# Layer 0 of a three-layer graph convolution sums its first 6 node tiles as dense count blocks

## The chip, the cores and the metric

The kernel runs on one core of a Trainium2 chip. The metric is the device time of one execution in microseconds, from which medians are taken. The engines are TensorE (PE, with its weight loads PEld), VectorE (DVE), ScalarE (ACT), GpSimd (POOL) and SyncE (SP), which issues plain DMAs.

## The reference

x has 6250 rows of 512 floats; `src` and `dst` list 106,250 edges (100,000 drawn ones and a loop at each node), sorted by `dst`. With deg the number of edges into a node and dinv = 1/sqrt(deg), each of three layers is

```python
msg = (h @ W)[src] * (dinv[src] * dinv[dst])[:, None]
h = segment_sum(msg, dst, n) + b
...
out = layernorm(x + h3)
```

The kernel uses that the layers are linear: y = dinv · h is summed over the edges, and W1·W2·W3 is applied as one product, once, at the end of layer 0. What remains of a layer is the sum of y[src] over each node's edges.

## The kernel before, in words

Nodes lie in 49 tiles of 128; `acc` holds them all in SBUF, and y of each layer is also stored in `y_dram`. A tile has about 16·128 = 2048 edges without its loops, and the loops are the start value of `acc`.

**Sparse sum.** The sorted edges are cut into 782 chunks of 128; 12 chunks make a group (66 groups) and 4 of them a quad (`CPQ`, 3 quads per group, `a` = 0, 1, 2). For each chunk POOL gathers 128 rows of y by an indirect DMA (line 808, `gather`), into a ring of 5 quads; `gather_quad(n)` waits until the quad 5 before is summed. PE multiplies a one-hot block of 32 columns with the gathered rows (`sum_quad`, line 1019), four chunks into four strips of one bank. After a group's last quad ACT copies the bank (`copy_slots`, line 1280), PE places the 128 rows by another one-hot product (`place_group`, line 1030), and DVE adds them, masked, to the two tiles that the group may touch (`add_group`, line 1648). DVE stages the one-hots: `stage_places` (line 1622, five quads ahead) and `stage_group` (line 1628).

**Dense sum.** In layers 1 and 2 the first 17 tiles are summed otherwise. `a_dram` holds for each of them a block of counts (uint8, how many edges go from each source node to each of the tile's nodes). A unit (`dense_unit`, line 1109) multiplies count blocks of 4 source tiles with their y rows, each row split in a high and a low float32r part (`high_part` on ACT, `low_part` on DVE, line 1789); ACT widens the counts (`widen_a`, line 1308), DVE adds the result to `acc` (`add_unit`, line 1800). Source tiles come back from `y_dram` by SP's loads (`load_y`, `load_a`). So in these layers only the groups from 22 on are gathered: 518 chunks, 131 quads.

**The count blocks are built in layer 0.** 272 windows of 8 nodes, 16 per tile: DVE stages two pairs of bf16 one-hots (`stage_window`, lines 1769 and 1770), PE multiplies them (`build_window`, line 1083), ACT copies the result into the tile's block (`keep_windows`, line 1288), SP stores the block (`store_a`). They are spread over quads 22 to 192 (`window_quad`), two build banks in turn. Ahead of them DVE finds the windows' edges, POOL gathers these (`gather_windows`, 6 indirect DMAs before the 14th quad), DVE turns them into values (`value_windows`, lines 1735 to 1753, at quad 17), and PE transposes these.

**Tiles of layer 0.** As a tile's last group is added, PE transposes it (`turn_done_tile`, line 1038), ACT copies it, PE multiplies it with W1·W2·W3 (`multiply_tile`, line 1054), DVE adds the bias (`bias_rows`, line 1656), ACT scales it (`scale_rows`, line 1248), and SP stores it. The last two tiles come after the loop (`last_tiles`). Layer 1's gathers wait until all tiles are stored.

**Order.** Every engine runs a list that is written out by quad: PE's `first_layer` in layer 0 does the sum of the quad, the placement of the group before, transposes, product, windows (line 1125); ACT's, DVE's and SP's have the same form (lines 1335, 1831, 695). An engine does its list in order, and each step waits on semaphores for its inputs; `FINISH` gives the quads of the tiles. Before the layer PE multiplies the weights (line 951) and turns the edge lists (`turn_lines`); `keep_groups` on DVE ends with the masks (`groups_ready`), for which POOL's first gather waits. Before quad 4 POOL waits for the weights and writes two constants (`window_consts`, line 812).

## Time and profile before

| | us |
|---|---|
| median of 3 runs | 2594.88 |
| lowest, highest | 2591.75, 2608.73 |
| profiled execution: span from first to last instruction | 2590.5 |
| profiled execution: its own time around the span | not recorded |
| layer 0, first to last gather | 137.4 to 1133.7 |
| layer 1, first gather | 1166.1 |

The profiled execution's own time is not among the results; its span is 1.2 us under the fastest of the three runs. Times in the profile are microseconds unless marked ns; PE, DVE, ACT, POOL and SP are the engines; an arrow points from what is read to what is written; the text behind an arrow in brackets names what ended an idle time.

### The profile page before, as it was taken

The numbers are of one execution on the slowest core, as the hardware profiler recorded it, in microseconds if no ns is written. First come the engines' busy times: TensorE is split into PE (matmuls) and PEld (weight loads), VectorE is DVE, ScalarE is ACT, GpSimd is POOL, SyncE is SP. The second block draws the span as 40 slices with busy tenths as digits, with TensorE's granted clock in tenths as the row PEclk, the third lists the DMA queues.
The fourth block names the chain that finished last, engine by engine and source line by source line (L and its number), as shares of the span: only waits on it lengthen the run. The fifth ranks groups of instructions, "written<-read, shape, count | busy, mean of one in ns | idle before, by whom it ended". The sixth has DMA issues, their size and how long they took to land. (4 is left out here: it accounts for less than half of the span.)

```text
span 2590.5 us, 30320 instructions
## 1 busy us (share of the span) xinstructions
PE 2035.3 (79%) x9476; PEld 998.1 (39%) x9476; DVE 1301.1 (50%) x3394; ACT 689.0 (27%) x1287; POOL 1767.1 (68%) x1864
## 2 busy tenths in 40 slices
PE   6565776777777767768998989998798888988854
PEld 6311222222222222225555555554355555555421
DVE  8323454445444544435444444445555555555577
ACT  0500222222222222223323223333322232223221
POOL 0267777777777777737777777777577776676652
PEclk9766888888878888889999999999899999999886
DMA  7667777777777778748888888889788888788784
GB/s 259 228 176 202 231 236 235 233 244 236 233 244 234 235 233 245 233 148 257 267 264 259 262 266 266 264 261 299 230 263 270 254 264 261 239 259 258 243 265 146
DMA packets 270364, 628.29 MB, mean 243 GB/s; under 512 B 46275, under 2 KB 99456, under 8 KB 270208
## 3 DMA queue, kind: packets, MB, share of 16 engines
q0 software_dynamic: 146256, 478.35, 61.3%
q1 hardware_dynamic: 123952, 148.03, 16.8%
q8 instruction: 77, 1.26, 0.2%
q14 instruction: 79, 0.65, 0.1%
HBM read 560.77 MB, written 65.45 MB: 242 GB/s over the span
## 5 line engine op out<-in xcount | busy, mean ns | idle before, releaser
L808 POOL DMA_INDIRECT ring<-y_dram,kept x1818 | 1741.0, 958 | 682.6 <-issue 575.1
L1019 PE MATMUL ps<-ring,onehot 128*32 128x512 f32 x3636 | 553.6, 679 | 302.6 <-DMA ring<-y_dram,kept 302.2
L1109 PE MATMUL ps<-dense_first,wide_a 128*128 128x512 f32 x1700 | 507.6, 421 | 49.5 <-DVE acc L1800 33.0
L1800 DVE SCALAR_TENSOR_TENSOR acc<-ps,acc 128x512 f32<-128x512 f32 x442 | 305.0, 690 | 360.1 <-PE ps L1109 350.4
L1109 PE MATMUL ps<-dense_next,wide_a 128*128 128x512 f32 x1224 | 382.1, 423 | 66.3 <-ACT wide_a L1308 39.0
L1109 PEld LDWEIGHTS ps<-dense_first,wide_a 128*128 128x128 f32 x1700 | 323.4, 196 | 218.9 <-issue 100.6
L1308 ACT CAST wide_a<-onehot 128x512 fp32r<-128x512 uint8 (+1 forms) x442 | 258.0, 594 | 372.9 <-PE ps L1109 366.5
L1622 DVE TENSOR_TENSOR onehot<-ps,kept 128x128 f32<-128x128 f32 x459 | 131.5, 287 | 412.8 <-PE ps L1019 412.7
L1109 PEld LDWEIGHTS ps<-dense_next,wide_a 128*128 128x128 f32 x1224 | 230.7, 194 | 202.9 <-issue 83.9
L1019 PEld LDWEIGHTS ps<-ring,onehot 128*32 128x32 f32 x3636 | 81.8, 113 | 498.8 <-issue 487.4
L1648 DVE SCALAR_TENSOR_TENSOR acc<-ps,mask,acc 128x512 f32 x308 | 217.0, 746 | 72.4 <-issue 67.4
L1769 DVE TENSOR_SCALAR onehot<-onehot 128x128 bf16<-128x128 bf16 x544 | 142.6, 262 | 192.6 <-PE ps L1083 192.2
L1280 ACT COPY onehot<-ps 128x512 f32<-128x512 f32 (+1 forms) x154 | 90.1, 585 | 556.1 <-PE ps L1019 556.1
L1054 PE MATMUL ps<-w,w_sb 128*128 128x512 f32 x376 | 220.5, 740 | 0.0
L1288 ACT CAST ring<-ps 128x392 uint8<-128x392 f32 x272 | 125.9, 486 | 316.6 <-PE ps L1083 314.6
L1030 PE MATMUL ps<-onehot 128*128 128x512 f32 (+1 forms) x308 | 190.8, 704 | 22.2 <-ACT onehot L1280 13.8
L1770 DVE TENSOR_SCALAR ring<-onehot 128x392 bf16<-128x392 bf16 x544 | 184.3, 339 | 0.0
L1083 PE MATMUL ps<-ring,onehot 128*128 128x392 bf16 x544 | 136.3, 358 | 31.9 <-DVE ring L1770 29.9
L1054 PEld LDWEIGHTS ps<-w,w_sb 128*128 128x128 f32 x376 | 86.6, 244 | 158.2 <-issue 158.2
L1109 PE MATMUL ps<-dense_last,wide_a 128*128 128x512 f32 x408 | 132.0, 406 | 0.0
L1248 ACT ACTIVATE acc<-h_sb,dinv 128x512 f32<-128x512 f32 x96 | 69.4, 722 | 191.2 <-DVE h_sb L1656 191.2
L1030 PEld LDWEIGHTS ps<-onehot 128*128 128x128 f32 (+1 forms) x308 | 49.8, 203 | 167.2 <-issue 167.2
(237 smaller groups left out, 1034.0 us busy)
## 6 DMA issues: line engine op xcount, KB each, us to landing
ring<-y_dram,kept POOLq DMA_INDIRECT x1818, 4.3
onehot<-a_dram SPq DMA_DIRECT2D x408, 64.0 KB
y_dram<-acc SPq DMA_DIRECT2D x99, 256.0 KB, 3.8
a_dram<-ring SPq DMA_DIRECT2D x17, 784.0 KB, 5.6
acc<-in_x_dram SPq DMA_DIRECT2D x1, 12288.0 KB
y_dram<-acc SPq DMA_DIRECT2D x12, 1024.0 KB, 10.8
ring<-y_dram SPq DMA_DIRECT2D x48, 256.0 KB, 4.8
out_dram<-row_sb SPq DMA_DIRECT2D x48, 256.0 KB
```

What stands on the lines that cost most here:

```text
L808: pool.indirect_dma_start(ring[:, s, :], None, y_dram[layer], bass.IndirectOffsetOnAxis(ap=rows, axis=0)).then_inc(done, 16)
L1019: mm = pe.matmul(ps[k * WIDE:(k + 1) * WIDE, g % BANKS, :], wide_hot[:, r, k, :], ring[:, r * CPQ + k, :], start=opens, stop=closes, tile_ ...
L1030: pe.matmul(ps[:, PLACE_BANK, :], place_hot[0:rows, g % 2, :], slots[0:rows, g % 2, :], start=True, stop=True).then_inc(placed, 1)
L1054: mm = pe.matmul(ps[:, PRODUCT_BANK, :], turned_sb[:, k * P:(k + 1) * P], w123[:, k, :], start=(k == 0), stop=(k == FB - 1))
L1083: mm = pe.matmul(ps[:, BUILD_BANKS[w % 2], 0:WIDTH], lo_hot[:, w % 2, h, :], v_hot[:, w % 2, h, :], start=(h == 0), stop=(h == 1))
L1109: mm = pe.matmul(ps[:, bank, :], wide_a[:, n % WIDE_SLOTS, P * k:P * (k + 1)], y_parts[(TILES * (layer - 1) + tile) % YSLOTS][:, part, :], ...
L1308: act.copy(wide_a[:, n % WIDE_SLOTS, 0:width], a_slots[n % ASLOTS][:, 0:width]).then_inc(a_ready, 1)
L1622: dve.tensor_tensor(wide_hot[:, n % RING_QUADS, :, :], iota_ps[:, 0:WIDE].unsqueeze(1).broadcast_to([P, CPQ, WIDE]), lo_f[:, c:c + CPW * ( ...
L1648: dve.scalar_tensor_tensor(out=rows, in0=ps[:, PLACE_BANK, :], scalar=mask[:, part, own:own + 1], in1=rows, op0=ALU.mult, op1=ALU.add).the ...
L1769: dve.tensor_scalar(lo_hot[:, w % 2, h, :], v_iota[:, HALF:HALF + P], lo_cols[:, at:at + 1], None, ALU.is_equal)
L1770: one = dve.tensor_scalar(v_hot[:, w % 2, h, :], v_iota, v_cols[:, at:at + 1], None, ALU.is_equal)
L1800: dve.scalar_tensor_tensor(out=rows, in0=ps[:, DENSE_BANKS[n % 2], :], scalar=0.5, in1=rows, op0=ALU.mult, op1=ALU.add).then_inc(dense_add ...
```

## The change

Layer 0 now sums its first 6 tiles (`EARLY_DENSE`) as dense count blocks as well, and gathers only from group 7 on: 698 chunks, 59 groups, 176 quads. To that end:
- The windows of these 6 tiles (96) are built first, three per quad in quads 11 to 42, the other 176 in quads 44 to 169. What leads to them is moved ahead: masks at quad 2 (was 5), search at 4 (was 8), window gathers before quad 10 (was 14), values at quad 8 (was 17). There is one build bank (5) in place of two, since the banks 3 and 6 go to the units. The first window of a quad stands before the quad's sum, the second behind it.
- 150 units (`dense0_unit`): 24 pairs of source tiles and a last single one, times 6 tiles, in quads 49 to 151. y rows are read back in pairs from `y_dram` (49 loads of 256 KB), count blocks in rows of 256 bytes (150 loads, 4 slots); ACT makes the high part and widens, DVE makes the low part and adds (`add0_unit`).
- The 6 tiles are finished at quads 151 to 161, and tiles finish at least two quads apart. The product of a tile uses the bank of its transposes, so `turn_done_tile` waits for the bias row before.
- The first 3 groups get masks of their own (`mask0`), which leave out what belongs to the 6 tiles; PE's weight products now stand behind a product that waits for `groups_ready`.
- b3 is loaded at the start of layer 1 in place of the start of the kernel, some SBUF regions are laid out anew, and the size of POOL's DMA scratch is given as 8192 bytes.

```diff
 DENSE_SPARE = 700
+EARLY_DENSE = 6
+PAIR = 2
+Y0_SLOTS = 4
+A0_SLOTS = 4
+WIDE0_SLOTS = 2
...
-    FIRST = [0, DENSE_GROUPS, DENSE_GROUPS]
...
-    WIN_AT = 22
-    WIN_QUADS = LAYER_QUADS[0] - WIN_AT - 4
+    WIN_AT = 11
+    WIN_PACE = 3
+    EARLY_WINDOWS = EARLY_DENSE * WPT
+    REST_AT = WIN_AT + EARLY_WINDOWS // WIN_PACE + 1
+    REST_QUADS = LAYER_QUADS[0] - REST_AT - 6
+    PAIRS0 = (TILES + PAIR - 1) // PAIR
+    UNITS0 = PAIRS0 * EARLY_DENSE
+    UNITS0_FROM = REST_AT + 5
+    UNITS0_TO = LAYER_QUADS[0] - 6 - 3 * EARLY_DENSE
...
+    def pair_of(b):
+        return range(PAIR * b, min(PAIR * b + PAIR, TILES))
+    UNIT0_QUAD = [UNITS0_FROM + (UNITS0_TO - UNITS0_FROM) * u // UNITS0 for u in range(UNITS0)]
+    LOAD0_QUAD = [UNITS0_FROM - 4 if b < 2 else UNIT0_QUAD[(b - 1) * EARLY_DENSE - 1] + 1 for b in range(PAIRS0)]
+    SPLIT0_QUAD = [UNITS0_FROM - 2 if b < 2 else LOAD0_QUAD[b] + 1 for b in range(PAIRS0)]
+    def units0_at(q):
+        return [u for u in range(UNITS0) if UNIT0_QUAD[u] == q]
+    def splits0_at(q):
+        return [k for k in range(TILES) if SPLIT0_QUAD[k // PAIR] == q]
...
     def finish_quads(layer):
-        dense = DENSE if layer > 0 else 0
-        sparse = [(first_quad(layer, LAST_GROUP[t] + 1) + (2 if layer == 0 else 0), 0, t) for t in range(dense, LOOP_TILES)]
-        return sorted(sparse + [(UNIT_QUAD[layer][UNITS - DENSE + t] + 1, 1, t) for t in range(dense)])
+        if layer > 0:
+            sparse = [(first_quad(layer, LAST_GROUP[t] + 1), 0, t) for t in range(DENSE, LOOP_TILES)]
+            return sorted(sparse + [(UNIT_QUAD[layer][UNITS - DENSE + t] + 1, 1, t) for t in range(DENSE)])
+        ready = sorted([(first_quad(0, LAST_GROUP[t] + 1) + 2, 0, t) for t in range(EARLY_DENSE, LOOP_TILES)]
+                       + [(UNIT0_QUAD[UNITS0 - EARLY_DENSE + t] + 3, 1, t) for t in range(EARLY_DENSE)])
+        found, at = [], -2
+        for q, late, t in ready:
+            at = max(q, at + 2)
+            found.append((at, late, t))
+        return sorted(found)
...
     def window_quad(w):
-        return WIN_AT + WIN_QUADS * w // WINDOWS
+        if w < EARLY_WINDOWS:
+            return WIN_AT + w // WIN_PACE
+        return REST_AT + REST_QUADS * (w - EARLY_WINDOWS) // (WINDOWS - EARLY_WINDOWS)
...
+            def load_y0(k):
+                if k == 0:
+                    sp.wait_ge(y0_stored, 16 * (X_BATCHES + 1))
+                    sp.wait_ge(win_values, 1)
+                if units0_before(k) > 0:
+                    sp.wait_ge(dense0_done, units0_before(k))
+                sp.dma_start(y0_raw[k % Y0_SLOTS], node_rows(y_dram[0], k, 0, P)).then_inc(y0_loaded[k % Y0_SLOTS], 16)
+            def load_a0(u):
+                b, t = divmod(u, EARLY_DENSE)
+                if u == 0:
+                    for k in range(2):
+                        sp.wait_ge(a_stored[k], 16 * ((EARLY_DENSE + 1 - k) // 2))
+                if u >= A0_SLOTS:
+                    sp.wait_ge(a0_ready, u - A0_SLOTS + 1)
+                width = P * len(pair_of(b))
+                sp.dma_start(a0_slots[u % A0_SLOTS][:, 0:width],
+                             a_dram[P * t:P * (t + 1), P * PAIR * b:P * PAIR * b + width]).then_inc(a0_loaded[u % A0_SLOTS], 16)
+            def load_dense0(q):
+                for b in range(PAIRS0):
+                    if LOAD0_QUAD[b] == q:
+                        for k in pair_of(b):
+                            load_y0(k)
+                if q == UNITS0_FROM - 2:
+                    for u in range(A0_SLOTS):
+                        load_a0(u)
+                for u in range(A0_SLOTS, UNITS0):
+                    if UNIT0_QUAD[u - A0_SLOTS] == q:
+                        load_a0(u)
             def store_a(q):
...
                     window_consts()
-                if n == WIN_AT - 8:
+                if n == WIN_AT - 1:
...
                 mm.then_inc(slots_ready, 1)
+                pe.wait_ge(first_ready, 1)
+                pe.wait_ge(groups_ready, 1)
+                pe.matmul(ps[:, GROUP_BANK, FIRST_AT:FIRST_AT + BOUNDARY], ones[0:1, :], first_tiles[0:1, :],
+                          start=True, stop=True).then_inc(first_spread, 1)
             def sum_quad(n):
...
             def turn_done_tile(t):
-                pe.wait_ge(added, 2 * (LAST_GROUP[t] + 1))
-                if t > 0:
-                    pe.wait_ge(turn_copied, t)
+                turn = TURN_OF[0][t]
+                if t < EARLY_DENSE:
+                    pe.wait_ge(dense0_added, UNITS0 - EARLY_DENSE + t + 1)
+                    pe.wait_ge(added, 2 * BOUNDARY)
+                else:
+                    pe.wait_ge(added, 2 * (GROUP.index((0, LAST_GROUP[t])) + 1))
+                if turn > 0:
+                    pe.wait_ge(turn_copied, turn)
+                    pe.wait_ge(h_ready, turn)
...
             def build_window(w):
                 pe.wait_ge(win_hot, w + 1)
-                if w > 1:
-                    pe.wait_ge(win_kept, w - 1)
+                if w > 0:
+                    pe.wait_ge(win_kept, w)
                 for h in range(2):
-                    mm = pe.matmul(ps[:, BUILD_BANKS[w % 2], 0:WIDTH], lo_hot[:, w % 2, h, :], v_hot[:, w % 2, h, :], start=(h == 0), stop=(h == 1))
+                    mm = pe.matmul(ps[:, BUILD_BANK, 0:WIDTH], lo_hot[:, w % 2, h, :], v_hot[:, w % 2, h, :], start=(h == 0), stop=(h == 1))
                 mm.then_inc(win_built, 1)
             def build(q):
-                if q == 7:
+                if q == 3:
                     sum_starts()
-                if q == WIN_AT - 4:
+                if q == WIN_AT - 2:
                     turn_windows(0)
-                if q == WIN_AT - 3:
+                if q == WIN_AT - 1:
                     turn_windows(1)
-                for w in windows_at(q):
-                    build_window(w)
+            def dense0_unit(u):
+                b, t = divmod(u, EARLY_DENSE)
+                bank = DENSE_BANKS[u % 2]
+                tiles = pair_of(b)
+                if t == 0:
+                    pe.wait_ge(split0_ready, tiles[-1] + 1)
+                pe.wait_ge(a0_ready, u + 1)
+                if u >= 2:
+                    pe.wait_ge(dense0_added, u - 1)
+                for k, tile in enumerate(tiles):
+                    for part in (y0_high, y0_low):
+                        mm = pe.matmul(ps[:, bank, :], wide0[:, u % WIDE0_SLOTS, P * k:P * (k + 1)], part[tile % Y0_SLOTS],
+                                       start=(k == 0 and part is y0_high), stop=(k == len(tiles) - 1 and part is y0_low))
+                mm.then_inc(dense0_done, 1)
...
                     g, a = QUAD[q]
+                    windows, units = windows_at(q), units0_at(q)
+                    for w in windows[:1]:
+                        build_window(w)
                     sum_quad(q)
+                    for w in windows[1:2]:
+                        build_window(w)
                     if a == 0 and q > 0:
                         place_group(g - 1)
                     for t in finished_at(0, q + 1):
                         turn_done_tile(t)
                     for t in finished_at(0, q):
-                        multiply_tile(t)
+                        multiply_tile(TURN_OF[0][t], TURN_BANK)
                     build(q)
+                    for w in windows[2:]:
+                        build_window(w)
+                    for u in units:
+                        dense0_unit(u)
             def last_tiles(layer):
                 place_group(GROUP_AT[layer + 1] - 1)
...
+                pe.wait_ge(dense0_added, UNITS0)
+                pe.wait_ge(h_ready, LOOP_TILES)
...
                 act.copy(y_parts[n % YSLOTS][:, 0, :],
                          y_rows[n % YSLOTS][:, 1, :] if tile > 0 else tile_of(source(0))).then_inc(high_ready, 1)
+            def high0(k):
+                act.wait_ge(y0_loaded[k % Y0_SLOTS], 16 * (k // Y0_SLOTS + 1))
+                if units0_before(k) > 0:
+                    act.wait_ge(dense0_done, units0_before(k))
+                act.copy(y0_high[k % Y0_SLOTS], y0_raw[k % Y0_SLOTS]).then_inc(high0_ready, 1)
+            def widen_a0(u):
+                width = P * len(pair_of(u // EARLY_DENSE))
+                act.wait_ge(a0_loaded[u % A0_SLOTS], 16 * (u // A0_SLOTS + 1))
+                if u >= WIDE0_SLOTS:
+                    act.wait_ge(dense0_done, u - WIDE0_SLOTS + 1)
+                act.copy(wide0[:, u % WIDE0_SLOTS, 0:width], a0_slots[u % A0_SLOTS][:, 0:width]).then_inc(a0_ready, 1)
             def widen_a(layer, u):
...
+                    windows = windows_at(q)
+                    for k in splits0_at(q):
+                        high0(k)
+                    keep_windows(windows[:1])
                     if q + 1 == QUADS_TO[g]:
                         copy_slots(g)
                     for t in finished_at(0, q + 1):
-                        keep_turned(t)
-                    keep_windows(q)
+                        keep_turned(TURN_OF[0][t])
+                    keep_windows(windows[1:])
+                    for u in units0_at(q + 1):
+                        widen_a0(u)
                     for t in finished_at(0, q):
-                        scale_rows(0, t)
+                        scale_rows(0, t, h_sb, TURN_OF[0][t])
...
+                                             scalar=float(EARLY_DENSE - part), in1=mask[:, part, EARLY_GROUPS:EARLY_GROUPS + BOUNDARY],
+                                             op0=ALU.is_ge, op1=ALU.mult).then_inc(mask0_ready, 1)
+                dve.wait_ge(mask0_ready, 2)
             def invert_degrees(twice):
...
+                    near = mask0[:, part, g:g + 1] if g < BOUNDARY else mask[:, part, own:own + 1]
+                    dve.scalar_tensor_tensor(out=rows, in0=ps[:, PLACE_BANK, :], scalar=near,
                                              in1=rows, op0=ALU.mult, op1=ALU.add).then_inc(added, 1)
             def bias_rows(layer, t, h=h_sb, bank=PRODUCT_BANK, turn=None):
...
             def build(q):
-                if q == 5:
+                if q == 2:
                     window_masks()
-                if q == 8:
+                if q == 4:
                     find_windows()
-                if q == WIN_AT - 5:
+                if q == WIN_AT - 3:
                     value_windows()
-                if q in (WIN_AT - 4, WIN_AT - 3):
-                    keep_columns(q - (WIN_AT - 4))
+                if q in (WIN_AT - 2, WIN_AT - 1):
+                    keep_columns(q - (WIN_AT - 2))
                 for w in windows_at(q + 1):
                     stage_window(w)
...
+                dve.wait_ge(high0_ready, k + 1)
+                dve.tensor_tensor(y0_low[k % Y0_SLOTS], y0_raw[k % Y0_SLOTS], y0_high[k % Y0_SLOTS].bitcast(F32),
+                                  ALU.subtract).then_inc(split0_ready, 1)
+            def add0_unit(u, groups):
+                dve.wait_ge(dense0_done, u + 1)
+                if groups > 0:
+                    dve.wait_ge(added, 2 * groups)
+                if u > 0:
+                    dve.wait_ge(dense0_added, u)
+                rows = tile_of(u % EARLY_DENSE)
+                dve.scalar_tensor_tensor(out=rows, in0=ps[:, DENSE_BANKS[u % 2], :], scalar=0.5, in1=rows,
+                                         op0=ALU.mult, op1=ALU.add).then_inc(dense0_added, 1)
             def add_unit(layer, u, groups):
...
                     g, a = QUAD[q]
+                    for u in units0_at(q - 1):
+                        add0_unit(u, g - (1 if a == 0 else 0))
                     finish_quad(q)
                     if a == 0 and q > 0:
                         add_group(g - 1)
                     build(q)
                     for t in finished_at(0, q):
-                        bias_rows(0, t)
+                        bias_rows(0, t, h_sb, TURN_BANK, TURN_OF[0][t])
+                    for k in splits0_at(q):
+                        low0(k)
             def last_tiles(layer):
...
-    nc = bacc.Bacc("TRN2", target_bir_lowering=False, num_devices=1)
+    nc = bacc.Bacc("TRN2", target_bir_lowering=False, num_devices=1, dynamic_dma_scratch_size=8192)
```

## Rows read from the trace of the kernel before

**Rows 1.** The page: busy time, share of the span and instructions of each engine.
```profile
PE 2035.3 (79%) x9476; PEld 998.1 (39%) x9476; DVE 1301.1 (50%) x3394; ACT 689.0 (27%) x1287; POOL 1767.1 (68%) x1864
```

**Rows 2.** Stretches: us, busy of PE, PEld, DVE, ACT, POOL, clock, DMA share, GB/s.
```profile
300.00:1100.00 800.00, 586.88 (x2339) 182.20 (x2340) 369.02 (x1354) 195.64 (x381) 607.40 (x633) 0.83 0.78 237
1200.00:1700.00 500.00, 455.28 (x2185) 271.84 (x2183) 238.61 (x427) 150.65 (x259) 379.24 (x397) 1.00 0.85 262
1700.00:1800.00 100.00, 88.60 (x427) 52.30 (x428) 51.82 (x92) 36.36 (x61) 75.75 (x80) 1.00 0.88 280
```

**Rows 3.** The gathers of line 808 in layer 0, and its waits (us, times).
```profile
L808 POOL DMA_INDIRECT ring<-y_dram,kept x782: 942/946/1627, 137.4 to 1133.7; - x196
...
  issue: 234.4, 770
...
  PE ps L1019: 3.4, 11
```

**Rows 4.** The gathers' wait for PE in layer 1 (us, times).
```profile
  PE ps L1019: 8.8, 29
```

**Rows 5.** The chain that ended last, in layer 2: start us, us, what.
```profile
1878.39 1.06 PE ps L1030 x2
...
1886.14 1.00 PE ps L1019 x8
1887.13 3.86 PE ps L1109 x16
```

**Rows 6.** Timeline, end of layer 0, PE: start us, us, engine line op.
```profile
1101.76 0.66 PE L1038 MATMUL ps<-ident,acc 128*128 128x128 f32 x4
...
1121.57 3.70 PE L1054 MATMUL ps<-w,w_sb 128*128 128x512 f32 x8
...
1125.11 0.83 PE L1083 MATMUL ps<-ring,onehot 128*128 128x392 bf16 x4
```

**Rows 7.** DVE lines of layer 1: count, min/median/max ns, first and last start.
```profile
L1800 DVE SCALAR_TENSOR_TENSOR acc<-ps,acc x197: 678/692/693, 1201.5 to 1797.7; 128x512 f32<-128x512 f32 x197
...
L1789 DVE TENSOR_TENSOR dense_first<-ring,dense_first x21: 680/684/766, 1216.5 to 1740.1; 128x512 fp32r<-128x512 f32 x21
```

**Rows 8.** Timeline, end of layer 0, DVE and ACT.
```profile
1088.19 0.24 DVE L1769 TENSOR_SCALAR onehot<-onehot 128x128 bf16<-128x128 bf16 x1
...
1088.59 0.24 DVE L1769 TENSOR_SCALAR onehot<-onehot 128x128 bf16<-128x128 bf16 x1
...
1127.10 0.28 DVE L1622 TENSOR_TENSOR onehot<-ps,kept 128x128 f32<-128x128 f32 x1
...
1128.03 0.35 DVE L1628 TENSOR_SCALAR onehot<-ps,kept 128x128 f32<-128x128 f32 x1 [0.65 <-PE ps L1030]
...
1128.36 0.48 ACT L1288 CAST ring<-ps 128x392 uint8<-128x392 f32 x1 [0.42 <-PE ps L1083]
...
1128.77 1.41 DVE L1648 SCALAR_TENSOR_TENSOR acc<-ps,mask,acc 128x512 f32 x2 [0.39 <-issue]
```

**Rows 9.** Timeline, start of layer 0.
```profile
133.81 16.34 PE L951 MATMUL ps<-ring 128*128 128x512 f32 x32
...
157.15 0.49 POOL L812 IOTA row_sb<- 128x392 f32 x1
...
240.92 0.55 DVE L1735 TENSOR_SCALAR ring<-ring 128x768 int32<-128x768 int32 x1
...
249.79 0.96 DVE L1753 TENSOR_TENSOR ring<-ring 128x768 f32<-128x768 f32 x1
```

**Rows 10.** Timeline, first gather of layer 1.
```profile
1166.12 0.94 POOL L808 DMA_INDIRECT ring<-y_dram,kept  x1 [31.47 <-issue]
```

**Rows 11.** DMA queues in layer 1 (packets, MB, share), and the count-block loads.
```profile
q0 software_dynamic: 36769, 120.51, 67.5%
q1 hardware_dynamic: 37998, 31.85, 17.1%
...
onehot<-a_dram SPq DMA_DIRECT2D x189, 64.0 KB
```

96 lines of the change are left out of this document (74 added, 22 removed).

## The prediction

> **What bounds the kernel now.** I read the engine totals first [rows 1]: PE is busiest with 79%, POOL second with 68%. That is an average over three layers, so next the table of stretches [rows 2]. The reader is to see that POOL does the same in both layers shown: 633 gathers in the 800 us of layer 0, 397 in 500 us and 80 in 100 us of layer 1, one per 1.26 us each time, although PE is 73% busy in the first and 91% in the second. Then line 808 alone [rows 3]. Its 782 gathers of layer 0 start between 137.4 and 1133.7 us. Nearly all its idle time (234.4 us over 770 gaps, 0.30 us each) is called issue: the gap of an engine that waits for nothing. It waits for PE (a free ring slot) 11 times, at most 0.3 us. So a gather costs 0.946 + 0.30 = 1.25 us, POOL never rests, and layer 0 is as long as its list of gathers. Layer 1 shows the same bound beside fuller PE work: between 1170 and 1800 us 29 waits for PE, 8.8 us in all [rows 4].
>
> **What is removed.** Layer 0 starts at group 7 (its first 6 tiles hold (128·16·6 − 700)/1536 = 7 whole groups), so 7 groups, 21 quads and 7·12 = 84 gathers go: 782 become 698, 197 quads become 176. Seven place products and fourteen additions go with them. At the pace of rows 3, (1133.7 − 137.4)/787 = 1.266 us per gather (781 steps and the 6 window gathers), stretches included: 84 · 1.266 = 106.3 us. All of it is on the path, if POOL stays the engine that never rests.
>
> **What is added, in PE time per quad.** A quad of four gathers lasts 4 · 1.266 = 5.06 us; this is the budget. The 150 units lie on quads 49 to 151, 1.46 per quad.
> - A unit is 4 products (2 source tiles, high and low part; 2 for the last block). 16 cost 3.86 us in layer 2 [rows 5], so 0.97 us; 1.41 us per quad.
> - Sum of the quad 1.00, a placement 1.07 per three quads, 0.36 [rows 5].
> - A tile's product 3.70 and its transposes 0.66 [rows 6], one tile per some 3.9 quads: 1.12.
> - Windows: two take 0.83 us [rows 6], 0.42 each; 176 over 126 quads, 1.4 per quad: 0.58.
> The sum is 1.00 + 0.36 + 1.12 + 0.58 + 1.41 = 4.47 us of 5.06, or 88%. Layer 1 runs at 91% PE busy and holds the pace of the gathers [rows 2], so the products as such fit.
>
> **DVE per quad:** 1.46 unit additions of 0.69 and half a low part of 0.68 [rows 7], 1.3; windows, two pairs of 0.40 each [rows 8], 1.4 · 0.80 = 1.1; one group addition per three quads, 0.65 + 0.35 + 0.39 + 1.41 [rows 8], 0.93; places 0.3, and a bias row like a unit addition, every 3.9 quads, 0.2. That is 3.9 of 5.06 us. It fits too, but DVE and PE are in order and hand work to each other, and here I expect the loss.
> - Quads 49 to 151: the first window of a quad is now built ahead of the sum. PE stands at it until DVE has staged it, and DVE stages it only after the group addition. Counted from the end of the units before: window 0.4, sum 1.0, place 1.07, to 2.5 us; DVE then 0.4 + 0.35 + 0.39 + 1.41 + 0.8, to 5.8 us; PE's own units end at 4.0. So PE idles 1.8 us in each group's first quad, unless a tile's product lies there. Behind the waiting window are the quad's sum and with it POOL's free slot. Three quads then need 3 · 4.47 + 1.8 = 15.2 us, and POOL gives them 15.2. This is break-even: I charge 0.05 us per quad over 103 quads, 5 us; bounds 0 (the tile's product fills the gap) and 0.3 per quad, 31 us.
> - Quads 11 to 42 carry three windows each (96 in 32 quads), and there is one build bank in place of two: each build waits for ACT's copy of the one before (0.48 us [rows 8]). Window w+2 needs the hot buffer of w, so DVE stages the last one only when PE has begun the next quad. By the same count a quad without a group takes 3.3 us, one with a group 6.6, and a tile's product adds 4.4 in four of five groups of quads: 16.7 per three, 5.6 each, 0.5 over the budget, 17 us in 32 quads. The ring of 5 quads absorbs some: a sum ends some 10 us after its first gather and its slot is wanted after 25, so PE may be 15 us late. It has about 7 us of lag already (next point). That leaves 17 + 7 − 15 = 9 us; bounds 0 and 24.
> - The window gathers move from the 14th to the 10th quad, and the values are wanted at quad 8. DVE will wait for their landing and then works 9.8 us (240.92 to 250.75 [rows 9]), with PE behind it at the transposes. The 6 gathers go out to about 196 us and land by 200, values are ready at 210, and POOL next needs a slot at about 221: nothing lost, but 7 us of lag.
> - Start: PE now waits for groups_ready before the weight products. These ran from 133.8 to 150.2 and would run from about 137 to 153.5; POOL asks for them at 157.15, before its IOTA [rows 9]. Hidden; without that cover 3 us. The small copies and masks on DVE lie before onehots wanted 5 us later; the one copy ahead of the masks costs 0.1 us. b3's load leaves the start and goes ahead of layer 1's tile loads: 0.4 us on SP, not on POOL's path.
> - End of layer 0: POOL stands 31.5 us until the last rows are stored [rows 10]. The last tile is finished at the same distance from the end (173 of 176, before 194 of 197), and the six early tiles at 151 to 161, before it. Same gap; I take 0, bounds −3 and +5.
> - SP: 49 tile loads and 150 count-block loads are queued with the stores of the tiles. They are issued two quads or more before use, 10 us; what is late next is ACT's widening. I charge 2 us, bounds 0 and 10.
>
> **DMA.** In layer 1, 461 gathers took 67.5% of 580 us, 0.85 us of all 16 engines each; the other queue took 17.1%, 99 us, for 189 count blocks (12.4 MB) and, from the rest of its 31.85 MB, 74 transfers of 256 KB. These at 0.85 are 63 us, which leaves 0.19 us per count block [rows 11]. Added in quads 49 to 151 (515 us): 49 · 0.85 + 150 · 0.19 = 70 us, a share of 0.14 on 0.78 [rows 2]: 0.92, where the rows hold the pace up to 0.88. I cost it at 0 in the sum; at the other end, a ceiling of 0.88 gives 515 · (0.92/0.88 − 1) = 23 us.
> The count blocks of layer 0 are read 256 bytes at a time, those of layer 1 512. The Trainium skill, DMA: Bandwidth & Descriptors, Specifications, says that below 512 bytes the engines read, modify and write and line rate is lost. No row here shows the two sizes apart. As a mechanism of this kernel, doubling the 0.19 gives 28 us more, a share of 0.98, and 515 · (0.98/0.88 − 1) = 58 us.
>
> The last edit gives POOL's queue 8192 bytes for its descriptors in place of the default. No row shows how many gathers either size holds. Four quads are under way at most and one gather lands while some four are issued, so I take 0; were it too small, POOL would wait for landings in all three layers, and one more gap of 0.30 us on 1734 gathers would be 520 us. I give that end 0.01 (in C's share).
>
> **Sum.** Against the profiled execution's span: 2590.5 − 106.3 + 5 + 9 + 2 = 2500. What lies around the span is not shown; the fastest run is 1.2 us above it and the median 4.4. I add 3: **2503 us**. Layers 1 and 2 keep their code; 0 there.
>
> **Rivals.**
> - A, DMA is the limit in quads 49 to 151. For it: shares rise to 0.92 or 0.98 with this traffic, and the ring has little room for later landings if PE lags as well. Against it: 0.88 held 80 gathers per 100 us [rows 2], and 84 gathers are gone. 2590.5 − 106 + 3 + (23 to 58), with the lock-step beside it: 2520 to 2550, say 2530.
> - B, TensorE stays at the mixed clock. It was granted 0.83 in layer 0 and 1.00 in layer 1 [rows 2]. PE's 587 us in 800 is 3.7 us per quad where the full clock's rows give 3.2: a factor of 1.15. Then 4.47 becomes 5.1, with the waits 5.6 us per quad, 0.55 · 103 = 57 us: 2545. Against it: idle waits for rows are what separates the layers, and these shrink.
> - C, slower than before: the one build bank. If every window's copy and its signals (0.48 + 0.4 us) stand open on PE instead of beside a sum or a product, PE needs 4.47 + 1.4 · 0.88 = 5.7 us per quad over 126 quads (+81), and 5.6 + 2.6 in the early 32 (+100): with 106 saved about 2590 + 75 = 2665. The change loses from about 0.67 us open per window on. For it: ACT's queue holds copies and widenings ahead of the next copy. Against it: the code puts the first window before the sum and the second behind it.
> - D, the gain is whole (the ring hides all): 2487.
>
> **Chances.** Forecast 0.55 (its own range 2492 to 2520), D 0.15, A 0.13, B 0.10, C 0.07. The range from 2482 to 2552 leaves out C and the edges of the others. One per cent is 26 us, about what a measurement of this kernel can tell from no change: faster by more than that (under 2569) are the forecast, D, A and most of B, 0.91; within, 0.04; slower 0.05.
>
> **What would show it.** Right: 698 gathers of line 808 in layer 0 at 1.25 to 1.29 us, the last at about 1042; the clock near 1.00 from quad 49 on; POOL waiting for PE some 10 us about 250 to 400 us and little later; PE waiting at the window product for DVE; the gap to layer 1 near 31 us. Wrong: gathers at 1.35 us or more in the second half of layer 0 with a DMA share at 0.9 (A), or with PE at 95% and a clock under 0.9 (B); PE idle on the build bank after ACT's window copy (C).

## The result, and the profile after

| us | before | changed | forecast |
|---|---|---|---|
| median | 2602.14 (6 runs) | 2577.57 (6 runs, 2568.29 to 2606.05) | 2503 (2482 to 2552) |
| ratio | | 0.9935 [0.9907, 0.9963] | 0.965 |
| profiled span | 2590.5 | 2603.8 | 2500 |
| last gather of layer 0 starts | 1133.7 | 1136.3 | 1042 |
| first gather of layer 1 starts | 1166.1 | 1170.1 | 1073.5 |

The kernel gains 0.65% by the ratio on record in place of 3.5%; the two medians in the table, divided, give 0.9906. The profiled execution is the slowest of its six, 28 us above their median. The lines of the new kernel that answer to [rows 3]: its gathers (line 919) of layer 0, with the first eight of layer 1, and the last two starts around the gap.

```profile
L919 POOL DMA_INDIRECT ring<-y_dram,kept x706: 940/946/2272, 137.6 to 1178.9; - x177
...
  issue: 195.7, 642
  PE ps L1134: 124.6, 62
```

```profile
1136.31 0.94 POOL L919 DMA_INDIRECT ring<-y_dram,kept  x1 [3.79 <-PE ps L1134]
1170.14 0.94 POOL L919 DMA_INDIRECT ring<-y_dram,kept  x1 [32.89 <-DMA y_dram<-acc]
```

84 gathers are gone, and the last one still starts 2.6 us later than before. A gather itself costs the same (0.946 + 0.30 us), so the new size of POOL's DMA scratch costs nothing that shows. What is new is 124.6 us in 62 waits for PE's sum to free a ring slot; before there were 3.4 us in 11. POOL no longer sets the pace.

Where that happens is read from the starts of every fourth gather (a quad has four), in us per quad; PE's busy and idle share of the same quads stand beside it, from its instructions in the trace.

| kernel | quads 20 to 49 (PE busy + idle) | quads 49 to 157 (PE busy + idle) | last gather |
|---|---|---|---|
| before | 5.09 (3.69 + 1.40) | 5.06 (3.70 + 1.36) | 1133.7 |
| changed | 7.18 (5.04 + 2.14) | 5.45 (4.53 + 0.92) | 1136.3 |

(7.18 − 5.09) · 29 = 61 us and (5.45 − 5.06) · 108 = 42 us: 103 us, nearly all of the 106 that was to be gained. The stretches behind it, before and changed in turn (us, busy of PE, PEld, DVE, ACT, POOL, clock, DMA share, GB/s):

```profile
225.00:420.00 195.00, 139.13 (x562) 44.33 (x558) 93.58 (x312) 42.64 (x82) 148.18 (x154) 0.84 0.77 230
480.00:960.00 480.00, 355.25 (x1413) 110.77 (x1414) 223.96 (x825) 118.47 (x230) 364.53 (x380) 0.83 0.78 236
```

```profile
225.00:420.00 195.00, 136.72 (x475) 40.64 (x474) 98.01 (x383) 50.66 (x101) 108.86 (x114) 0.74 0.62 184
480.00:960.00 480.00, 400.85 (x1778) 182.68 (x1776) 303.68 (x852) 166.51 (x362) 340.27 (x351) 0.94 0.81 249
```

In the first stretch (three windows per quad) PE is as busy as before and does a quarter fewer sums; the clock fell to 0.74. In the second (the units) the clock rose to 0.94, where near 1.00 was forecast, and the DMA share is 0.81. PE's and POOL's waits in these stretches (us, times, longest), first 225 to 420, then 480 to 960:

```profile
PE ps L1204 <- ACT ring L1436: 33.9, 35, 1.9
PE ps L1204 <- DVE ring L1953: 24.4, 9, 3.8
POOL ring L919 <- PE ps L1134: 56.1, 22, 6.9
...
PE ps L1204 <- DVE ring L1953: 59.2, 35, 2.8
PE ps L1204 <- ACT ring L1436: 19.1, 15, 5.6
PE ps L1227 <- DVE acc L1989: 0.7, 2, 0.4
POOL ring L919 <- PE ps L1134: 39.7, 22, 5.8
```

PE waits nearly always at one place, the window product (line 1204): for DVE's one-hots (line 1953), and for ACT's copy out of the one bank (line 1436). The units themselves (line 1227) wait 0.7 us in 480. One round of three early quads on PE (start, us, line, wait before), and the stretches in it by clock (the clock is the first number behind POOL's brackets):

```profile
284.34 1.06 PE L1134 MATMUL ps<-ring,onehot 128*32 128x512 f32 x8
...
285.68 1.02 PE L1145 MATMUL ps<-onehot 128*128 128x512 f32 x2
...
289.73 0.83 PE L1204 MATMUL ps<-ring,onehot 128*128 128x392 bf16 x2 [2.70 <-DVE ring L1953]
290.49 1.94 PE L1134 MATMUL ps<-ring,onehot 128*32 128x512 f32 x8
292.36 0.84 PE L1204 MATMUL ps<-ring,onehot 128*128 128x392 bf16 x2
292.99 1.06 PE L1159 MATMUL ps<-ident,acc 128*128 128x128 f32 x4
295.20 0.81 PE L1204 MATMUL ps<-ring,onehot 128*128 128x392 bf16 x2 [1.16 <-ACT ring L1436]
296.68 0.81 PE L1204 MATMUL ps<-ring,onehot 128*128 128x392 bf16 x2 [0.67 <-ACT ring L1436]
297.43 1.94 PE L1134 MATMUL ps<-ring,onehot 128*32 128x512 f32 x8
...
299.92 4.99 PE L1175 MATMUL ps<-w,w_sb 128*128 128x512 f32 x8
...
305.91 0.49 PE L1204 MATMUL ps<-ring,onehot 128*128 128x392 bf16 x2 [0.67 <-ACT ring L1436]
306.33 1.07 PE L1134 MATMUL ps<-ring,onehot 128*32 128x512 f32 x8
```

```profile
284.34:289.10 4.76, 2.69 (x15) 0.78 (x14) 3.15 (x10) 1.46 (x3) 3.70 (x4) 1.00 0.80 235
289.10:302.70 13.60, 11.15 (x34) 3.52 (x35) 6.57 (x29) 3.50 (x7) 8.24 (x9) 0.50 0.71 217
302.70:309.50 6.80, 4.28 (x19) 1.35 (x19) 2.61 (x10) 1.58 (x3) 2.92 (x4) 1.00 0.45 120
```

From sum to sum of the same place in the group the round takes 22.0 us, where POOL would need 15.2. The place product at 285.68 opens the longest wait: DVE adds the group only then, and stages the next window behind that. During that wait of 2.70 us the granted clock fell from 1.00 to 0.50 and came back at 302.7: the two sums in between take 1.94 us each in place of 1.06, and the tile's product, more than half of its time at the low clock, 4.99 in place of 3.70. The sum at 306.33 takes 1.07 us again, although PE waited 0.67 us just before it.

### The profile page after: what moved, and what is told of

It reads as the page before. It is cut to its first block and busy times, and to the rows that moved or that the text cites. A ratio compares the mean times of both kernels' runs of the same rounds, so it can differ in the third digit from the quotient of the medians.

```text
span 2603.8 us, 32039 instructions
## 1 busy us (share of the span) xinstructions
PE 2122.2 (82%) x9884; PEld 1096.7 (42%) x9884; DVE 1421.8 (55%) x3556; ACT 761.5 (29%) x1479; POOL 1688.9 (65%) x1780
## 5 line engine op out<-in xcount | busy, mean ns | idle before, releaser
L919 POOL DMA_INDIRECT ring<-y_dram,kept x1734 | 1662.8, 959 | 775.0 <-issue 508.4
L1134 PE MATMUL ps<-ring,onehot 128*32 128x512 f32 x3468 | 517.7, 666 | 75.9 <-DMA ring<-y_dram,kept 75.4
L1244 PE MATMUL ps<-dense_first,wide_a 128*128 128x512 f32 x1700 | 515.3, 426 | 53.3 <-DVE acc L2000 32.4
L1204 PE MATMUL ps<-ring,onehot 128*128 128x392 bf16 x544 | 159.6, 380 | 187.7 <-DVE ring L1953 118.5
L1830 DVE SCALAR_TENSOR_TENSOR acc<-ps,mask,acc 128x512 f32 x294 | 207.2, 746 | 78.5 <-issue 73.6
L1145 PE MATMUL ps<-onehot 128*128 128x512 f32 (+1 forms) x294 | 178.2, 690 | 20.2 <-ACT onehot L1428 13.9
L1204 PEld LDWEIGHTS ps<-ring,onehot 128*128 128x128 bf16 x544 | 35.9, 101 | 362.2 <-DVE ring L1953 224.7
L1134 PEld LDWEIGHTS ps<-ring,onehot 128*32 128x32 f32 x3468 | 74.4, 112 | 256.8 <-issue 250.6
L1175 PE MATMUL ps<-w,w_sb 128*128 128x512 f32 x376 | 182.0, 629 | 0.0
L1809 DVE TENSOR_SCALAR onehot<-ps,kept 128x128 f32<-128x128 f32 x147 | 51.4, 350 | 141.3 <-PE ps L1145 141.1
```

The source lines that it names most:

```text
L919: pool.indirect_dma_start(ring[:, s, :], None, y_dram[layer], bass.IndirectOffsetOnAxis(ap=rows, axis=0)).then_inc(done, 16)
L1134: mm = pe.matmul(ps[k * WIDE:(k + 1) * WIDE, g % BANKS, :], wide_hot[:, r, k, :], ring[:, r * CPQ + k, :], start=opens, stop=closes, tile_ ...
L1145: pe.matmul(ps[:, PLACE_BANK, :], place_hot[0:rows, g % 2, :], slots[0:rows, g % 2, :], start=True, stop=True).then_inc(placed, 1)
L1175: mm = pe.matmul(ps[:, bank, :], turned_sb[:, k * P:(k + 1) * P], w123[:, k, :], start=(k == 0), stop=(k == FB - 1))
L1204: mm = pe.matmul(ps[:, BUILD_BANK, 0:WIDTH], lo_hot[:, w % 2, h, :], v_hot[:, w % 2, h, :], start=(h == 0), stop=(h == 1))
L1244: mm = pe.matmul(ps[:, bank, :], wide_a[:, n % WIDE_SLOTS, P * k:P * (k + 1)], y_parts[(TILES * (layer - 1) + tile) % YSLOTS][:, part, :], ...
```

## The experiments

Each kernel is the changed kernel with the edit that is shown; e0 and e11 are without one. A pace is the time per quad, for quads 20 to 49 and 49 to 157. The runs e0 to e3 were made on one chip (before: 2594.53 us median), f1 to f3 on another with 2595.59 us. For e4 to e7 the kernel before took 2945.69 us, for e8 to e11, on a third chip, 2942.88 us; these eight are compared by their ratios alone.

**e0: the changed kernel again.**

> The changed kernel once more, as it is. It was 0.65% faster than the kernel before (0.9935), and its profiled execution was the longest of its six. Theory H (hand-overs): in layer 0 POOL waits for PE because PE stands for ACT's window copy (one build bank), for DVE's staging and behind ACT's wait for y rows. Then this profile shows again over 6.5 us per quad while quads 11 to 44 are summed and 5.3 to 5.5 us in the units' quads. Rival L (luck): the 105 us that went missing belong to that one slow execution, and this profile shows layer 0 at 5.1 us per quad and the last gather near 1030 us. Time by H: 2565 to 2580 us, by L the same here but with the profile 80 us shorter in layer 0.

Measured: 2588.76 us (12 runs, 2574.70 to 2601.49), 0.9977 [0.9958, 0.9997]. Paces 7.06 and 5.42: the loss is there again, at a median somewhat above the 2565 to 2580 us expected. By the two ratios the change is worth 0.2 to 0.65%.

**e1: two banks for the 96 early windows.**

```
+        def build_bank(w):
+            return 6 if w < EARLY_WINDOWS and w % 2 == 0 else BUILD_BANK
-                if w > 0:
+                if 1 < w < EARLY_WINDOWS:
+                    pe.wait_ge(win_kept, w - 1)
+                elif w > 1:
                     pe.wait_ge(win_kept, w)
...
```

(PE's product and ACT's copy take `build_bank(w)` in place of `BUILD_BANK`.)

> The first 96 windows are built in two banks in turn (bank 5 and bank 6, which the units take only from quad 49 on), so that a build waits for the copy of the window two before. Theory bank: PE stood 33.9 us for ACT's copy between 225 and 420 us, at a clock of 0.74; without that the early stretch falls from 7.1 to about 6 us per quad, 30 us shorter, 2545 us. Rival staging: DVE's staging behind the group addition and PE's low clock set the pace of the early stretch, and the waits only move to DVE: 0 to 10 us shorter. Rival DMA predicts no change.

Measured: 2534.40 us (2530.74 to 2536.19), 0.9765 [0.9750, 0.9781]. Stretch 225 to 420, and the window products in it (count, busy, mean ns of one, idle before them):

```profile
225.00:420.00 195.00, 150.15 (x662) 50.61 (x660) 129.95 (x494) 66.82 (x141) 148.38 (x154) 0.89 0.81 250
```

```profile
L1210 PE MATMUL ps<-ring,onehot 128*128 128x392 bf16 x202 | 55.0, 367 | 45.8 <-DVE ring L1959 30.4 <-ACT ring L1442 15.5
```

The early quads are back at 5.09 us with 154 gathers, as many as before; those from 49 on stay at 5.38, as they must. The second bank gives 54 us against e0, where about 30 were expected, and by the paces nearly all of it early (57 us, and 4 later). Not all of it is time spent waiting for the bank: the granted clock of the stretch is 0.89 in place of 0.75 too. DVE's waits did not shrink (30.4 us, 23.4 in e0, over more quads), so they alone did not make the early loss.

**e2: y rows split two quads after their load in place of one.**

```
-    SPLIT0_QUAD = [UNITS0_FROM - 2 if b < 2 else LOAD0_QUAD[b] + 1 for b in range(PAIRS0)]
+    SPLIT0_QUAD = [UNITS0_FROM - 2 if b < 2 else LOAD0_QUAD[b] + 2 for b in range(PAIRS0)]
```

> The high and low parts of a pair of y rows (from the third pair on) are made one quad later, two quads after their load is issued instead of one. Theory load: ACT stands at the landing of the y rows (31 us in all between 480 and 960 us, up to 4.7 us at a time), with the copy of the quad's first window behind it and PE behind that (19.1 us of waits for the copy, 5.6 at most). Then these waits go and the units' quads fall by 15 to 25 us in all, 2550 to 2560 us. Rival staging: the loss in the units' quads is PE's 59 us of waits for DVE's window staging; then 0 to 5 us. Rival transfer limit: the loads land late because the DMA engines are full, and the waits stay with a quad more or less: 0.

Measured: 2567.20 us (2556.63 to 2588.66), 0.9918 [0.9889, 0.9946]. What it acts on, ACT and PE of the changed kernel:

```profile
708.65 0.62 ACT L1454 CAST x_rows<-w_sb 128x512 fp32r<-128x512 f32 x1 [4.66 <-DMA w_sb<-y_dram]
712.22 0.62 ACT L1454 CAST above_dense<-w_sb 128x512 fp32r<-128x512 f32 x1 [2.95 <-DMA w_sb<-y_dram]
712.74 0.48 ACT L1436 CAST ring<-ps 128x392 uint8<-128x392 f32 x1
```

```profile
706.21 0.51 PE L1204 MATMUL ps<-ring,onehot 128*128 128x392 bf16 x2 [1.80 <-DVE ring L1953]
...
713.36 0.81 PE L1204 MATMUL ps<-ring,onehot 128*128 128x392 bf16 x2 [5.65 <-ACT ring L1436]
```

ACT stands at a y row that has not landed, with the copy of a window that PE built 6.5 us earlier queued behind it, and PE stands at the bank. With the later split PE's waits for ACT between 480 and 960 us fall from 20.4 (e0) to 4.3 us, and the pace from 5.42 to 5.32: 11 us over 108 quads, between the two expectations (15 to 25, 0 to 5). The rest of e2's gain isn't the edit's. Its quads 20 to 49 hold the same instructions as e0's and ran at 6.21 in place of 7.06; see the last section.

**e3: DVE stages the next quad's first window ahead of the group addition.**

```
...
+                    early = windows_at(q + 1)[:1] if q >= WIN_AT else []
+                    for w in early:
+                        stage_window(w)
                     if a == 0 and q > 0:
                         add_group(g - 1)
-                    build(q)
+                    build(q, len(early))
```

> DVE stages the first window of the next quad ahead of the addition of a finished group, from quad 11 on; the rest of its order is kept. Theory staging: PE stands at a quad's first window for DVE (24.4 us between 225 and 420 us in 9 waits, 59.2 us between 480 and 960 us in 35), behind the group addition of about 2.9 us; these waits fall to a third, and the time by 40 to 60 us, to 2520 to 2535 us. Rival bank: the early stretch keeps its pace, since PE then stands for ACT's copy: 15 to 25 us. Rival load: no more than 10 us.

Measured: 2504.78 us (2501.81 to 2507.36), 0.9654 [0.9639, 0.9669]. The two stretches, then POOL's waits in the second:

```profile
225.00:420.00 195.00, 137.81 (x598) 44.37 (x598) 117.66 (x462) 64.15 (x129) 136.01 (x141) 0.90 0.75 231
480.00:960.00 480.00, 421.36 (x1922) 189.66 (x1914) 323.03 (x923) 177.66 (x389) 365.00 (x378) 0.96 0.85 266
```

```profile
POOL ring L919 <- PE ps L1134: 0.6, 2, 0.3
```

(`build` then leaves out what is staged already.) Six changed lines that add no instruction give 84 us back against e0, more than the 40 to 60 us expected. PE's waits for DVE's one-hots in 480 to 960 fall from 59.2 (e0) to 14.1 us; those for ACT's copy rise from 20.4 to 35.5 us and do no harm. From quad 49 on the pace is 5.09: 378 gathers in 480 us against 380 before, POOL waits for PE 0.6 us, and DMA at a share of 0.85 holds that. The early quads go from 7.06 to 5.66, at a clock of 0.90 in place of 0.75.

**f1: PE builds the first window behind the quad's sum.** It tests the step of the prediction by name: is it the sum that stands behind a late window?

```
-                    for w in windows[:1]:
-                        build_window(w)
                     sum_quad(q)
+                    for w in windows[:1]:
+                        build_window(w)
```

> The changed kernel, with the first window of a quad behind the quad's sum on PE instead of ahead of it; DVE's order and the one bank stay. If the loss is the sum, and with it POOL's free slot, standing behind a window product whose one-hots DVE stages late (theory 1 as the prediction put it), the quads from 49 on fall from 5.4 to about 5.1 us (108 quads, some 35 us) and the early ones from 7.1 by the 1 us or so that PE stands there per quad: 2520 to 2550 us, ratio 0.97 to 0.98. If it is the length of the whole round (the place product behind the windows, the group addition behind the place product, the staging behind that), the order on PE only shifts it: early quads stay at 7 us or more and the ratio within 0.99 to 1.00; it may rise, since two windows then stand back to back on one bank.

Measured: 2552.05 us (2542.29 to 2562.77), 0.9822 [0.9790, 0.9853]. PE's and POOL's waits, 225 to 420 and 480 to 960:

```profile
PE ps L1204 <- ACT ring L1436: 44.0, 38, 2.9
PE ps L1204 <- DVE ring L1953: 11.6, 9, 1.8
POOL ring L919 <- PE ps L1134: 49.7, 19, 4.4
...
PE ps L1204 <- ACT ring L1436: 39.5, 36, 5.8
PE ps L1204 <- DVE ring L1953: 28.2, 29, 2.5
POOL ring L919 <- PE ps L1134: 7.2, 11, 3.1
```

The two theories share the layer between them. From quad 49 on (5.17 in place of 5.42) POOL's wait goes from 39.7 to 7.2 us: there the sum behind the window was the loss, as the step said. In the early quads (6.85 in place of 7.06, 0.2 us where 1 was expected) DVE's waits only turned into ACT's and POOL still loses 49.7 us: there the whole round is too long, and this order on PE does not mend it.

**f2: two banks, and staging ahead** (the edits of e1 and e3 together).

> Two banks for the early windows and staging ahead of the group addition. If the two losses are separate, quads 20 to 49 run at 5.1 us where staging alone left 5.66: 16 us below it, ratio 0.959 where the kernel before takes 2595 us (2489 us). If staging alone already frees what the bank cost (the 5.66 being a slower clock or lag): ratio 0.965. Where the kernel before takes some 2945 us, 0.973 to 0.978 as measured there, and (b) stays open.

Measured: 2496.47 us (2495.65 to 2498.28), 0.9622 [0.9604, 0.9641], the fastest of all; it beats both kernels.

```profile
225.00:420.00 195.00, 142.04 (x657) 48.46 (x655) 124.79 (x488) 66.80 (x142) 148.99 (x152) 0.93 0.80 248
480.00:960.00 480.00, 419.55 (x1910) 187.81 (x1909) 322.28 (x921) 176.14 (x384) 365.06 (x378) 0.96 0.85 264
```

```profile
PE ps L1138 <- DMA ring<-y_dram,kept: 23.9, 15, 6.6
PE ps L1210 <- ACT ring L1442: 16.1, 17, 1.3
PE ps L1210 <- DVE ring L1959: 12.9, 18, 1.9
...
POOL ring L923 <- PE ps L1138: 0.9, 3, 0.3
```

Quads 20 to 49 run at 5.15, 49 to 157 at 5.09, and PE's sums wait for gathered rows again, as before (waits of 225 to 420 us). The layer is bound by POOL's list once more. The ratio lies between the two that were expected (0.959, 0.965). The two gains overlap: 54 and 84 us alone, about 92 together (0.9977 − 0.9622 of 2595). The paces against e0 say where: in the early quads 57 (e1), 41 (e3) and 55 us (f2), in the later ones 4, 36 and 36. The early loss is mended by either edit, most of all by the bank, the later one by the staging alone; and 5.06 us per quad, POOL's own pace before, is the floor of both.

**f3: staging ahead, and the first window behind the sum.**

> Staging ahead of the group addition, and the first window behind the sum on PE; one bank. If staging ahead is what pays and PE's order is then without weight: ratio 0.965 as with staging alone. If the window ahead of the sum was useful (it gives the one bank's copy the whole sum to hide behind), the early quads rise from 5.66 to 6 us or more: 10 us or more above, ratio 0.969 or higher.

Measured: 2504.52 us, 0.9657 [0.9637, 0.9678]; paces 5.57 and 5.10, as e3. Once DVE stages ahead, the order on PE has no weight that can be told.

**e4 to e11, where every kernel was 13% slower.**

e6 copies the second window ahead of ACT's copies of a transposed tile; e7 builds two early windows per quad:

```
+                    keep_windows(windows[1:2])
                     for t in finished_at(0, q + 1):
                         keep_turned(TURN_OF[0][t])
-                    keep_windows(windows[1:])
+                    keep_windows(windows[2:])
...
-    WIN_PACE = 3
+    WIN_PACE = 2
```

e4 and e8 are f2's kernel, e5 and e9 add e2's edit to it, e10 is e3's and e6's edit with one bank, e11 the changed kernel.

> The two early build banks and the earlier staging of a quad's first window together. Apart they gave 0.9765 and 0.9654 of the time before. Theory hand-overs: bank and staging are the whole early loss, staging alone the loss in the units' quads; then quads 20 to 49 go at 5.1 us and the later ones at 5.1, the last gather starts near 1030 us, 2488 us. Rival, DMA as a limit: beside the units a pace of 5.2 us or more stays however well the engines hand over, 2500 us. Rival, one remedy makes the other moot: no better than the earlier staging alone, 2505 us.

> The three edits together: two early banks, earlier staging, high and low parts a quad later. Theory hand-overs: POOL never waits long in layer 0, the whole 106 us of the gathers appear, 2485 us, equal to the two edits together within 3 us, since the ring hides ACT's waits for y rows once PE has slack. Rival load: ACT's waits for the rows (35.5 us on PE, 7.2 at most, with the earlier staging) still cost, and this kernel beats the two edits by 5 to 10 us.

> The changed kernel with one swap on ACT: it copies a quad's second window before the turned tile, as PE makes them in that order. One build bank stays. Theory bank: PE's waits for ACT in the early stretch (33.9 us) come mostly from the copy itself (0.48 us and two signals per window), so 5 to 10 us of them go, 2578 us. Rival order: they come from copies that stand behind the turned tile in ACT's list (waits of up to 1.9 us, one per tile); then 20 us or more go, 2565 us or less.

> Two windows per quad instead of three in the first 96, in quads 11 to 58; the units then start at quad 65 and come 1.7 per quad. The bank and the staging order stay. Theory hand-overs: each window of a quad costs its hand-over, so with two a quad takes some 5.3 us in place of 7.1, and the early stretch gives back 50 us, while the denser units (PE needs 4.7 us per quad and waits for DVE in each group's first quad) lose 10 to 25 us more: 2550 us. Rival clock: the early stretch is slow because PE idles and falls to the lower clock; with fewer windows it idles no less, and the time stays at 2580 us.

> Two banks for the early windows, and DVE stages the next quad's first window ahead of a group addition; on a chip where the kernel before takes some 2595 us. If the two hand-overs are what was lost (theory 1), the edits add up: staging alone gave 2505 us with quads 20 to 49 at 5.66 us each, two banks take these to 5.1 (29 quads times 0.55, 16 us): 2489 us, ratio 0.959. If both edits only bring PE's clock or its lag back (theory 2), the first is enough and the second adds nothing: 2505 us, ratio 0.965. If the DMA engines are the limit from quad 49 on (rival A), the quads become 5.3 us or more there as the early ones shorten: 2510 us or more.

> As the run with both edits, and y-row splits one quad later after their loads. If ACT's standing at the landings is a third loss of its own: 3 to 8 us below the run with two edits (quads 49 to 157 at 5.03 in place of 5.09). If it was only harmful while PE was late for other reasons: within 3 us of it.

> One bank stays. DVE stages ahead of the group addition, and ACT copies the second window of a quad ahead of the transposed tile's copies instead of behind them. If what the early quads still lose beside the staging is the bank's wait for ACT's copies behind other work: quads 20 to 49 at 5.1 to 5.4 and 2490 to 2500 us, ratio near 0.961. If it is the plain product, copy, signal cycle of three windows in one bank: quads 20 to 49 stay at 5.6 and 2505 us, ratio 0.965.

> The changed kernel without an edit, as the measure for the other three: 2570 to 2605 us, ratio 0.993 to 1.00 against the kernel before. With granted clock near 0.9 in 225 to 300 us it comes out near 2570, with 0.75 there near 2590 or above.

| | ratio | quads 20 to 49 | 49 to 100, 100 to 157 |
|---|---|---|---|
| e11 changed | 0.9903 [0.9879, 0.9928] | 7.10 | 6.27, 6.07 |
| e6 copy first | 0.9827 [0.9799, 0.9855] | 6.57 | 6.30, 6.03 |
| e7 two per quad | 0.9825 [0.9799, 0.9850] | 6.17 | 6.20, 6.46 |
| e4 two edits | 0.9746 [0.9721, 0.9772] | 5.94 | 6.01, 6.06 |
| e8 two edits | 0.9765 [0.9743, 0.9787] | 5.96 | 6.15, 6.05 |
| e5 three edits | 0.9735 [0.9707, 0.9762] | 5.84 | 6.01, 6.14 |
| e9 three edits | 0.9764 [0.9745, 0.9783] | 6.09 | 6.19, 6.18 |
| e10 stage, copy first | 0.9761 [0.9737, 0.9784] | 6.10 | 6.09, 6.03 |

The expectations in microseconds don't apply at this speed, and e11 came out below its 0.993. By ratios, e6 and e7, which relieve the one bank in two ways, lie some 0.8% under e11; this compares two chips, and their intervals come within 0.3% of one another, so it is weak evidence. With staging ahead it is 1.4% (e8 and e10 against e11, one chip). e7 moves the windows later, and its last quads pay (6.46). The third edit adds nothing to two that can be told (e5 to e4, e9 to e8); e10 equals e8, but whether one bank would do at the usual speed isn't told by that, since what POOL loses here to unknown stops (last section) is far more than the edits differ by.

## Why the prediction was wrong

**The bound and what is removed: right.** POOL's list was the limit. With the hand-overs mended (f2) the last gather starts at 1033.2, 100.5 us earlier, for 106.3 forecast. The start (137.6), the gap (33.8 us in place of 32.4) and the work as such also hold: PE was forecast at 4.47 us of products per quad from 49 on and has 4.53. The 3 us for what lies around the span are 2.2 to 2.4 in the six runs. Whatever else the change moved (SBUF places, the weight products, the scratch size) costs little, since f2 keeps it all and is 99 us faster than the kernel before.

**The early quads, charged 9 us: this step failed, 61 us.** Its round was 16.7 us per three quads: 11.3 of products and 5.4 of waits. In the trace the waits are 3 · 2.14 = 6.4, near that. The products take 3 · 5.04 = 15.1 us, a third more than the prices of [rows 5, 6] gave: here the granted clock was 0.74. The cross-check is f2, where the same products take 3 · 3.55 = 10.7 us at a clock of 0.93. So the round is 15.1 + 6.4 = 21.5 us and not 16.7, and 3.8 of the 4.8 us too much are the products' price: over 29 quads 37 us by the price and 10 by the waits. The ring's slack, 8 us, was then soon gone. Rival B's factor of 1.15, from the 0.83 of the kernel before, would have priced the products at 13.0 us. The Trainium skill, TensorE: Matmul & The Clock Gate, HAM oscillation, describes a kernel whose waits for DMA return the array to half clock in each iteration. This trace agrees in part: its waits are for other engines, and the clock fell to 0.50 during the wait of 2.70 us. That the waits as a whole set the clock is not shown: e2 has the same code and the same idle time per quad as e0 up to quad 48, and a clock of 0.88 for 0.75 (last section). Rival B had a low clock as its mechanism, but was looked for only beside the units, where it was 0.94.

**The lock-step beside the units, charged 5 us (bounds 0 and 31): failed by size, 42 us.** The forecast wait for DVE was 1.8 us per group; 59.2 us in 480 (29 groups) are 2.0. The mechanism was right, and the error was to charge it at break-even, which leaves no room for anything else. There was something: 19.1 us of waits for ACT's copy, 0.65 per group, which the forecast did not have. 3 · (4.53 + 0.92) = 16.35 us per group stand against 15.2: 0.65 of the difference is ACT's, 0.2 DVE's, 0.2 the products'. e3 shows that the wait for DVE's staging decides (5.09 with 14.1 us of it left, though PE waits longer for ACT), e2 that ACT's part is 0.1 us per quad, f1 that the harm passes through the sum behind the window.

**The loads, charged 2 us: wrong by a fact of the code.** "Issued two quads or more before use" holds where the use is the unit on PE, but ACT comes first: from the third pair on it splits the y rows one quad after their load, and it widens a count block one or two quads after its load. A y-row load took 5.3 and 5.7 us in the median (480 to 960), about a quad, and ACT's queue carries window copies behind it (e2: 11 us for the y rows).

**Rivals.** A (DMA): not seen. At full pace (e3, f2) the share is 0.85, not 0.92 or 0.98. SP's queue from 480 to 960 us, in the kernel before and in f2 (packets, MB, share):

```profile
q1 hardware_dynamic: 4700, 13.41, 7.1%
q1 hardware_dynamic: 28512, 27.47, 17.4%
```

It took 10 points more where 14 were forecast, and the queue of the gathers fell from 70.8 to 67.0% for as many gathers (380, 378). The forecast gave each count block the 0.19 us of layer 1's blocks, which are twice as large (64 KB, here 32). In f2's packet records 119 blocks took 17.7 us of all 16 engines, 0.15 each. The Trainium skill, DMA: Bandwidth & Descriptors, Specifications, puts line rate at transfers of at least 512 bytes. The trace agrees in part: a packet of 256 bytes took 18 ns in the median and one of 512 bytes (kernel before, 1250 to 1750 us) 27, a third more per byte, and nothing like the doubled time that the rival priced.

C (the one bank) was the right place with the wrong price: by the prediction it needed 0.67 us open per window to lose (0.60 when its own sums are redone); the early windows have 33.9 us in 195, 81 windows, 0.42 each, and the later ones 0.16. The losses fall on one chain, so C, the lock-step and the clock together took what none was thought to take alone. D (the ring hides all) is what f2 comes near: 2496 for 2487.

**Signs.** Right: PE waiting at the window product for DVE; the number of gathers; the gap; roughly the clock beside the units (0.94 for near 1.00). Wrong: the last gather (1136.3 for 1042); the pace, with gathers 1.36 us apart from quad 49 on and none of A's and B's other signs (share 0.81, clock 0.94); POOL's wait for PE early on, 56.1 us in 225 to 420 where some 10 were forecast.

## What to carry to other kernels

Two engines in order that hand work back and forth have a round of their own; write that round down over one full period and compare it with the pacemaker's, and where the two come out equal, charge the round's uncertainty, not zero. Price TensorE's work in a stretch with waits at the clock that the nearest such stretch of the trace was granted, not at the full clock, and keep room for a lower one. Before adding work to a filled list, ask of each producer whether its next output stands behind something long that doesn't need it: here one staging step moved ahead of one addition was worth 84 us, where the whole change had brought 6 us in the same comparison (0.23% of 2595).

## What the runs showed of the hardware

**The same instructions get another clock from execution to execution.** Up to quad 48 e2 and e0 do the same work in the same order. Stretch 225 to 420 of e0, then of e2:

```profile
225.00:420.00 195.00, 135.85 (x479) 41.70 (x478) 98.69 (x385) 52.16 (x104) 110.95 (x116) 0.75 0.62 186
```

```profile
225.00:420.00 195.00, 127.69 (x534) 39.54 (x534) 109.90 (x427) 57.35 (x116) 122.61 (x129) 0.88 0.68 203
```

PE's idle time per quad (20 to 49) is equal (2.11 and 2.08 us), its busy time isn't (4.95 and 4.12): 0.83 us per quad, 24 us over 29 quads, with nothing but the clock to tell them apart. What sets it is open. That fits the spread of the kernels: 27 us over twelve runs of e0, 38 over six of the changed kernel, but 5.6 us for e3 and 2.6 for f2. In the twelve runs of e0 the clock over the whole execution is 0.918 in the fastest and 0.897 in the slowest, though not in strict order between; the same cause in all of them is argued, not shown.

**At times every kernel was 13% slower.** It was so on the two chips of e4 to e7 and e8 to e11. By the chip numbers on record the first of them is also that of f1 to f3, run later at the usual 2595.59 us, so it isn't a property of the chip. In these runs all engines stand together at times. e11 in layer 1:

```profile
1422.39 1.52 DVE L2000 SCALAR_TENSOR_TENSOR acc<-ps,acc 128x512 f32<-128x512 f32 x2 [5.48 <-remote]
1422.44 1.14 ACT L1471 CAST wide_a<-onehot 128x512 fp32r<-128x512 uint8 x2 [4.27 <-remote]
...
1423.52 0.95 POOL L919 DMA_INDIRECT ring<-y_dram,kept  x1 [3.65 <-remote]
```

"Remote" marks a release whose sender the profile doesn't show; POOL lost 244.0 us to it in the whole execution, and nothing in e0; its gathers take the same 0.946 + 0.30 us. What it is stays open. The gains of the edits shrink there (1.4% for f2's kernel, e8 against e11, and 3.6% at the usual speed). Beside the units the pace goes from 5.42 to 5.09 us at the usual speed, and from 6.17 to 6.09 here. That stops of POOL leave the other engines time to catch up would explain it, and is argued.
